# Attention slots with the two probability transposes half a slot apart, and the bias sums split

## The chip, the cores and the metric

One core of one Trainium2 chip. The metric is the device time of one launch in microseconds, the median of several runs.

## The reference

The input is x, 32 sequences of 256 rows of 128 numbers. The output is x plus two branches of its layernorm: attention and a mixture of experts. All is fp32.

```python
xn = layernorm(x)
out = x + attention(xn) + ffn(xn)

# attention, 16 heads of 64
Q = xn @ Wq + bq;  K = xn @ Wk;  V = xn @ Wv;  R = xn @ Wr + br      # R: 10 numbers per head and row
extra[b,h,t,p] = sum_n R[b,h,t,n] * b_nd[n, t-p]   where 0 <= t-p < 128, else the logit is -1e9
W = softmax(Q K^T / 8 + extra);   A = W V;   return A @ Wproj + bproj

# ffn: 8 experts of 512, the two best per row by router logits, gelu, softmax-weighted sum
```

The window makes each block of 128 query rows look at one or two blocks of 128 keys: per head 128 x 128 numbers for the first query block (t = 0) and 128 x 256 for the second (t = 1), 384 columns in all.

## The kernel before

After a preparation (weights turned and split, layernorm, routing) the kernel runs attention for sequences 0 to 15, then the expert blocks, then attention for sequences 16 to 31. Each pass of 16 sequences is written as a first sequence, a hardware loop of seven turns with two sequences each, a last sequence, and a tail of four slots.

**Slots.** A sequence has eight slots j, one per pair of heads. Each engine has a function `sequence` that writes out its own order of work; engines meet by semaphores alone. In slot j, TensorE (lines 1428 to 1444) does:

- `keys` (lines 1281 to 1283): queries and keys of pair j + 1, six matmuls, into the bank KEY_BANK. ScalarE copies them to `qk` (line 776).
- `units` at place 0: in slots 0, 2, 3 and 5 a quarter of the values ("v", copied by ScalarE to `val`, line 757), in slots 1 and 4 an "r" unit (copied to `r_raw` at line 763, rounded on POOL at line 641, remainder on VectorE at line 1064, called `weights` there).
- `logits` of pair j (line 1392) into one of two pairs of banks.
- in even slots `values` (line 1412), the product of turned probabilities and values for the quad of heads that ended with pair j - 3; in odd slots `outputs` (line 1422), its projection.
- `turn_probs` (line 1381), three transposes of one head's probabilities, for the first ("even") head of pair j - 2, into the one bank PT_BANK.
- `units` at place 1: a position unit "g" (line 1352), in every slot. VectorE copies it to `gst` (line 1057), SP writes that to memory and reads it back skewed as `extra` (lines 468 and 480), the bias for a later slot.
- `turn_probs` of the second ("odd") head of pair j - 2, into the same bank.

All v, r and g units share one bank, MISC_BANK, and wait for the copy of the unit before.

**VectorE** (lines 1077 to 1113) in slot j: reciprocal of the sums of pair j - 1 (line 1083); four reductions `tensor_tensor_reduce` (line 1093), which add `extra` to the logits and keep the minimum, two for t = 0, then two for t = 1; in odd slots `add_heads` (line 1122), the sum of an output quad; `copy_probs` (line 1073) of the even head of pair j - 2; the copy of the position unit; `copy_probs` of the odd head; in slots 1 and 4 `weights`. In the second pass `add_rows` (line 1136), four instructions, stands behind slots 1 and 2 and adds expert results.

`turn_probs` and `copy_probs` wait for each other, as there is one bank:

```python
pe.wait_ge(norm_made, 2 * (i * H + h + 1))     # turn_probs
wait_from(pe, pT_made, i * H + h)
...
dve.wait_ge(pT_psum, i * H + h + 1)            # copy_probs
wait_from(dve, head_psum, i * QUADS + h // 4)  # the values that read this buffer
```

**ScalarE** (lines 779 to 802) in slot j: copy of the keys; copy of the v or r unit; exponents of the pair (line 792), two for t = 0, two for t = 1, each with an accumulator read; in even slots the copy `headT` of the values' bank (line 801).

**POOL**: `split_q` for the next sequence in slot 0 (lines 630 to 635), the four scalings of pair j - 1 by its reciprocals (lines 666 and 668), and eight indirect DMAs per sequence (lines 651 and 653), which move rows to and from the experts. Its order and SP's are the same before and after.

## Time and profile before

| what | value |
|---|---|
| median of 3 runs | 1775.75 us (1775.34 to 1776.92) |
| profiled execution | 1773.52 us, of which the span is 1771.7 us |
| mean granted TensorE clock | 0.972 |
| busy over the span | TensorE 85%, VectorE 58%, ScalarE 54%, POOL 45% |
| two attention passes | about 137 to 810 us and 1087 to 1770 us |
| expert blocks | about 810 to 1087 us |

Times in the rows are microseconds from the start of the span unless marked ns. PE is TensorE's matmul side, PEld its weight loads, DVE is VectorE, ACT ScalarE, POOL GpSimd, SP SyncE. "Idle before" is time in which an engine did nothing ahead of an instruction, with the instruction that ended it behind the arrow; "issue" means that the profile shows no releaser. A wait on a register's value is often named so, whoever ended it.

### The profile page before, as it was taken

How to read it: one execution, taken by the hardware profiler on the slowest of the kernel's cores; microseconds unless marked ns; L12 is line 12 of the kernel's file. 1: busy time of each engine (PE TensorE's matmuls, PEld its weight loads, DVE VectorE, ACT ScalarE, POOL GpSimd, SP SyncE). 2: the span in 40 equal slices, each digit the busy share in tenths (PEclk: the TensorE clock that was granted, in tenths of full speed). 3: DMA queues.
4: the chain of work that ended last, by engine and by line, in shares of the span. 5: the costliest groups of instructions: out<-in, count | busy, mean ns of one | idle time of the engine just before them, and what ended most of it. 6: DMA issues, size and time to landing. Idle time of an engine off the chain costs nothing.

```text
span 1771.7 us, 43010 instructions
## 1 busy us (share of the span) xinstructions
PE 1497.9 (85%) x11335; PEld 1150.4 (65%) x11335; DVE 1026.8 (58%) x3715; ACT 956.8 (54%) x2864; POOL 804.7 (45%) x1515
## 2 busy tenths in 40 slices
PE   2556888888888888888999998888888888888886
PEld 1224666666666666667999996666666666666665
DVE  4675666666666666663212122676666766766675
ACT  1223566555666666664444453666665665655654
POOL 0323555655555555561000001555665565655554
PEclk8687999999999999999999998999999999999999
DMA  9765554545545554544666665555555555555541
GB/s 282 276 238 149 153 146 145 150 144 150 157 139 145 148 148 139 149 127 132 200 208 200 209 197 165 145 149 137 153 148 144 150 148 139 153 146 150 147 137 48
DMA packets 375831, 283.10 MB, mean 160 GB/s; under 512 B 16634, under 2 KB 349988, under 8 KB 375716
## 3 DMA queue, kind: packets, MB, share of 16 engines
q1 hardware_dynamic: 367524, 265.16, 50.7%
q0 software_dynamic: 8192, 16.79, 3.6%
q14 instruction: 90, 0.74, 0.1%
q8 instruction: 25, 0.41, 0.1%
HBM read 168.57 MB, written 113.26 MB: 159 GB/s over the span
## 4 chain that ended last, share of the span: by engine, by line
PE 61%; DVE 17%; issue 15%; SPq 4%; DMA 1%; DVEq 1%; POOL 0%; ACT 0%; POOLq 0%; ACTq 0%
PE ps L1381 11%; PE ps L1412 9%; PE ps L1317 8%; PE ps L1281 8%; PE ps L1392 7%; PE ps L1282 7%; PE ps L1283 7%; DVE probT L1073 7%; DVE logit L1093 5%; PE ps L1422 2%; DVE low L1093 1%; PE ps L1299 1%; SPq L435 1%; SPq L396 1%; PE ps L1352 1%
## 5 line engine op out<-in xcount | busy, mean ns | idle before, releaser
L792 ACT ACTIVATE prob<-logit,low 128x128 f32<-128x128 f32 (+1 forms) x1024 | 453.7, 444 | 264.0 <-DVE low L1093 260.1
L1093 DVE CUSTOM_DVE_ANT_0 logit<-ps,extra 128x128 f32<-128x128 f32 (+1 forms) x1024 | 306.3, 355 | 313.1 <-issue 237.9
L1381 PE MATMUL ps<-ident,prob 128*128 128x128 f32 x1536 | 265.7, 282 | 166.7 <-DVE probT L1073 145.1
L666 POOL TENSOR_SCALAR prob<-prob,inv 128x128 f32<-128x128 f32 x512 | 188.4, 368 | 437.9 <-DVE inv L1083 436.7
L1073 DVE COPY probT<-ps 128x384 f32<-128x384 f32 x512 | 284.3, 555 | 110.3 <-PE ps L1381 62.9
L1381 PEld LDWEIGHTS ps<-ident,prob 128*128 128x128 f32 x1536 | 165.1, 141 | 261.1 <-issue 200.1
L776 ACT COPY qk<-ps 128x512 f32<-128x512 f32 x256 | 150.0, 586 | 251.0 <-PE ps L1283 249.6
L668 POOL TENSOR_SCALAR prob<-prob,inv 128x256 f32<-128x256 f32 x512 | 241.2, 471 | 0.0
L1392 PE MATMUL ps<-qk 64*128 64x128 f32 (+1 forms) x2048 | 237.2, 350 | 0.0
L1412 PE MATMUL ps<-probT,val 128*64 128x256 f32 (+1 forms) x2048 | 194.7, 332 | 2.7 <-issue 1.4
L792 ACT ACTIVATION_READ_ACCUMULATOR prob<-logit,low 128x1 f32 x1024 | 191.5, 187 | 0.0
L1057 DVE COPY gst<-ps 128x512 f32<-128x512 f32 x256 | 174.4, 681 | 13.1 <-DMA skew<-gst 7.8
L1412 PEld LDWEIGHTS ps<-probT,val 128*64 128x64 f32 x2048 | 127.1, 136 | 81.5 <-issue 42.3
L1392 PEld LDWEIGHTS ps<-qk 64*128 64x128 f32 x2048 | 134.2, 186 | 65.1 <-ACT qk L776 36.0
L641 POOL CAST r_hi<-r_raw 120x512 fp32r<-120x512 f32 x64 | 39.0, 610 | 300.7 <-ACT r_raw L763 300.7
L1281 PE MATMUL ps<-xq_hi,wqk_hi 128*128 128x256 f32 x512 | 165.7, 324 | 1.4 <-ACT qk L776 1.4
L1422 PEld LDWEIGHTS ps<-wproj,headT 128*128 128x128 f32 x1024 | 123.9, 191 | 43.0 <-issue 41.2
L651 POOL DMA_INDIRECT x_place<-xrow,at_now x128 | 131.9, 1031 | 38.5 <-issue 25.3
L1422 PE MATMUL ps<-wproj,headT 128*128 128x128 f32 x1024 | 148.1, 288 | 1.4 <-ACT headT L801 1.4
L1317 PEld LDWEIGHTS ps<-w2b,hid 128*128 128x128 f32 x1248 | 145.2, 192 | 3.3
L653 POOL DMA_INDIRECT yget<-y_place,at_now x128 | 129.9, 1015 | 36.5 <-issue 24.9
L1317 PE MATMUL ps<-w2b,hid 128*128 128x128 f32 x1248 | 145.4, 275 | 0.0
(171 smaller groups left out, 2425.2 us busy)
## 6 DMA issues: line engine op xcount, KB each, us to landing
skew<-gst SPq DMA_DIRECT2D x256, 256.0 KB
extra<-skew SPq DMA_DIRECT2D x128, 512.0 KB, 3.8
extra<-skew SPq DMA_DIRECT2D x128, 256.0 KB, 2.9
w1b<-w_d SPq DMA_DIRECT2D x39, 514.0 KB, 3.5
w2b<-w_d SPq DMA_DIRECT2D x39, 320.0 KB, 3.3
x_place<-zero SPq DMA_DIRECT2D x39, 256.0 KB, 2.8
placed<-x_place SPq DMA_DIRECT2D x39, 256.0 KB, 3.7
y_place<-yrow SPq DMA_DIRECT2D x39, 256.0 KB, 2.2
```

What stands on the lines that cost most here:

```text
L666: nc.gpsimd.tensor_scalar(prob[:, h, 0:P], prob[:, h, 0:P], inv[:, h, 0:1], 1.0, ALU.mult, ALU.mult).then_inc(norm_made, 1)
L668: nc.gpsimd.tensor_scalar(prob[:, h, P:], prob[:, h, P:], inv[:, h, 1:2], 1.0, ALU.mult, ALU.mult).then_inc(norm_made, 1)
L792: ins = nc.scalar.activation(prob[:, h % PB, a:b], logit[:, h % LB, a:b], ACT.Exp, scale=-1.0, bias=low[:, h % LB, t:t + 1], accum_out=tot ...
L1057: nc.vector.tensor_copy(gst[:, t, :], ps[:, MISC_BANK, :]).then_inc(g_made, 1)
L1073: nc.vector.tensor_copy(probT[:, h % 4, :], ps[:, PT_BANK, 0:3 * P]).then_inc(pT_made, 1)
L1093: ins = nc.vector.tensor_tensor_reduce(out=logit[:, h % LB, a:b], in0=ps[:, S_BANK[j % 2][n], a:b], in1=extra[:, h, a:b], scale=1.0, scala ...
L1281: nc.tensor.matmul(dst, a_hi, b_hi, start=start, stop=False)
L1317: mm = nc.tensor.matmul(ps[:, Y_BANK[u], t * P:(t + 1) * P], hid[:, u, c, t * P:(t + 1) * P], w2b[:, u, c * P:(c + 1) * P], start=(c == 0) ...
L1381: mm = nc.tensor.transpose(ps[:, PT_BANK, n * P:(n + 1) * P], prob[:, h % PB, n * P:(n + 1) * P], ident[:, :])
L1392: mm = nc.tensor.matmul(ps[:, S_BANK[pair % 2][n], cols], qk[rows, pair % 2, 0, q], qk[rows, pair % 2, 1, k], start=True, stop=True)
L1412: mm = nc.tensor.matmul(ps[DQ * n:DQ * n + DQ, HEAD_BANK, q], val[:, s, v:v + DQ], probT[:, hh % 4, p], start=(s == 0), stop=(s == 1), ski ...
L1422: mm = nc.tensor.matmul(ps[:, HEAD_BANK, t * E:(t + 1) * E], headT[:, pair, t * P:(t + 1) * P], wproj[:, (2 * quad + pair) % PAIRS, :], st ...
```

## The change

Only the order of instructions on three engines changes; each instruction, bank and buffer stays.

- TensorE: logits of pair j; place-0 unit; transposes of the odd head of pair j - 3; keys of pair j + 1; position unit; transposes of the even head of pair j - 2; values or outputs.
- VectorE: `weights` of the slot before (so now in slots 2 and 5); copy of the odd head of pair j - 3; reductions for t = 0; reciprocal of pair j - 1; reductions for t = 1; copy of the position unit; copy of the even head of pair j - 2; `add_heads`; `add_rows`.
- ScalarE: place-0 unit; keys; exponents for t = 0; `headT`; exponents for t = 1.

```diff
@@ -776,23 +776,26 @@
                 nc.scalar.copy(qk[:, pair % 2, :, :].rearrange("p n k -> p (n k)"),
                                ps[:, KEY_BANK, :]).then_inc(key_made, 1)
 
+            def exponents(i, j, t):
+
+                a, b = ((0, P), (P, 3 * P))[t]
+                act.wait_ge(logit0_made if t == 0 else logit_made, i * PAIRS + (j + 1))
+                for h in (2 * j, 2 * j + 1):
+                    if t == 0:
+                        wait_from(act, pT_psum, i * H + (h + 1 - PB))
+                    ins = nc.scalar.activation(prob[:, h % PB, a:b], logit[:, h % LB, a:b], ACT.Exp,
+                                               scale=-1.0, bias=low[:, h % LB, t:t + 1],
+                                               accum_out=total[:, h % PB, t:t + 1])
+                return ins
+
             def sequence(i, start, heads=True, more=True):
                 for j in range(PAIRS if heads else LAG):
+                    for n, kind, k, t, ahead in units_at(j, 0, more) if heads else []:
+                        unit(len(START) + i * len(UNITS) + n, kind, k, t, i + ahead)
                     if heads and (j + 1 < PAIRS or more):
                         keys(i if j + 1 < PAIRS else i + 1, (j + 1) % PAIRS)
-                    for n, kind, k, t, ahead in units_at(j, 0, more) if heads else []:
-                        unit(len(START) + i * len(UNITS) + n, kind, k, t, i + ahead)
                     if heads:
-                        for t, (a, b) in enumerate(((0, P), (P, 3 * P))):
-                            act.wait_ge(logit0_made if t == 0 else logit_made, i * PAIRS + (j + 1))
-                            for h in (2 * j, 2 * j + 1):
-
-                                if t == 0:
-                                    wait_from(act, pT_psum, i * H + (h + 1 - PB))
-                                ins = nc.scalar.activation(prob[:, h % PB, a:b], logit[:, h % LB, a:b], ACT.Exp,
-                                                           scale=-1.0, bias=low[:, h % LB, t:t + 1],
-                                                           accum_out=total[:, h % PB, t:t + 1])
-                        ins.then_inc(prob_made, 1)
+                        exponents(i, j, 0)
                     if j % 2 == 0 and here(i, j - 4, heads, start):
 
                         quad = (j - 4) // 2
@@ -800,6 +803,8 @@
                         wait_from(act, out_psum, i * QUADS + quad)
                         nc.scalar.copy(headT[:, :, :].rearrange("p n t -> p (n t)"),
                                        ps[:, HEAD_BANK, :]).then_inc(head_made, 1)
+                    if heads:
+                        exponents(i, j, 1).then_inc(prob_made, 1)
 
             def experts(b, u, k):
                 if not isinstance(b, int) or b + 1 < PLACES:
@@ -1072,43 +1077,49 @@
                 wait_from(dve, head_psum, i * QUADS + h // 4)
                 nc.vector.tensor_copy(probT[:, h % 4, :], ps[:, PT_BANK, 0:3 * P]).then_inc(pT_made, 1)
 
+            def reduce(i, j, t):
+
+                a, b = ((0, P), (P, 3 * P))[t]
+                for n in range(2):
+                    h = 2 * j + n
+                    ins = nc.vector.tensor_tensor_reduce(
+                        out=logit[:, h % LB, a:b], in0=ps[:, S_BANK[j % 2][n], a:b], in1=extra[:, h, a:b],
+                        scale=1.0, scalar=BIG, op0=ALU.add, op1=ALU.min, accum_out=low[:, h % LB, t:t + 1])
+                ins.then_inc(logit0_made if t == 0 else logit_made, 1)
+
             def sequence(i, start, heads=True, more=True):
                 for j in range(PAIRS if heads else LAG):
-                    pair = j - 1
-                    if here(i, pair, heads, start):
-
-                        h = 2 * pair % PB
-                        dve.wait_ge(prob_made, i * PAIRS + pair + 1)
-                        wait_from(dve, norm_made, 2 * (i * H + 2 * pair + 2 - PB))
-                        nc.vector.reciprocal(inv[:, h:h + 2, :], total[:, h:h + 2, :]).then_inc(inv_made, 1)
+                    for n, kind, k, t, ahead in units_at(j - 1, 0, more) if heads else []:
+                        if kind == "r":
+                            weights(i + 1, k)
+                    if here(i, j - 3, heads, start):
+                        copy_probs(i, 2 * (j - 3) + 1)
                     if heads:
                         if j % 2 == 0:
                             wait_apart(dve, skew_in[j], (i + 1) * 16, const_made)
                             dve.wait_ge(skew_in[j + 1], (i + 1) * 16)
                         wait_apart(dve, s_psum, i * PAIRS + j + 1, const_made)
                         wait_apart(dve, prob_made, i * PAIRS + j + 1 - LB // 2, const_made)
-                        for t, (a, b) in enumerate(((0, P), (P, 3 * P))):
-                            for n in range(2):
-                                h = 2 * j + n
-                                ins = nc.vector.tensor_tensor_reduce(
-                                    out=logit[:, h % LB, a:b], in0=ps[:, S_BANK[j % 2][n], a:b], in1=extra[:, h, a:b],
-                                    scale=1.0, scalar=BIG, op0=ALU.add, op1=ALU.min, accum_out=low[:, h % LB, t:t + 1])
-                            ins.then_inc(logit0_made if t == 0 else logit_made, 1)
-                    if j % 2 == 1 and here(i, j - 5, heads, start):
-                        add_heads(i, (j - 5) // 2)
+                        reduce(i, j, 0)
+                    pair = j - 1
+                    if here(i, pair, heads, start):
+
+                        h = 2 * pair % PB
+                        dve.wait_ge(prob_made, i * PAIRS + pair + 1)
+                        wait_from(dve, norm_made, 2 * (i * H + 2 * pair + 2 - PB))
+                        nc.vector.reciprocal(inv[:, h:h + 2, :], total[:, h:h + 2, :]).then_inc(inv_made, 1)
+                    if heads:
+                        reduce(i, j, 1)
+                    for n, kind, k, t, ahead in units_at(j, 1, more) if heads else []:
+                        positions(len(START) + i * len(UNITS) + n, i + ahead, k, t)
                     if here(i, j - 2, heads, start):
                         if isinstance(i, int) and i == HALF and j == 2:
 
                             dve.wait_ge(y_out[0], (PLACES + 1) // 2 * 16)
                             dve.wait_ge(y_out[1], PLACES // 2 * 16)
                         copy_probs(i, 2 * (j - 2))
-                    for n, kind, k, t, ahead in units_at(j, 1, more) if heads else []:
-                        positions(len(START) + i * len(UNITS) + n, i + ahead, k, t)
-                    if here(i, j - 2, heads, start):
-                        copy_probs(i, 2 * (j - 2) + 1)
-                    for n, kind, k, t, ahead in units_at(j, 0, more) if heads else []:
-                        if kind == "r":
-                            weights(i + 1, k)
+                    if j % 2 == 1 and here(i, j - 5, heads, start):
+                        add_heads(i, (j - 5) // 2)
                     if j in ADDS and start == HALF and here(i, -1, heads, start) and heads:
                         add_rows(i - HALF - 1, ADDS.index(j), i - 1)
 
@@ -1427,21 +1438,21 @@
 
             def sequence(i, par, start, heads=True, more=True):
                 for j in range(PAIRS if heads else LAG):
+                    if heads:
+                        logits(i, j)
+                        units(i, par, j, 0, more)
+                    if here(i, j - 3, heads, start):
+                        turn_probs(i, 2 * (j - 3) + 1)
                     if heads and (j + 1 < PAIRS or more):
                         keys(i if j + 1 < PAIRS else i + 1, par if j + 1 < PAIRS else 1 - par, (j + 1) % PAIRS)
                     if heads:
-                        units(i, par, j, 0, more)
-                        logits(i, j)
+                        units(i, par, j, 1, more)
+                    if here(i, j - 2, heads, start):
+                        turn_probs(i, 2 * (j - 2))
                     if j % 2 == 0 and here(i, j - 4, heads, start):
                         values(i, (j - 4) // 2)
                     if j % 2 == 1 and here(i, j - 5, heads, start):
                         outputs(i, (j - 5) // 2)
-                    if here(i, j - 2, heads, start):
-                        turn_probs(i, 2 * (j - 2))
-                    if heads:
-                        units(i, par, j, 1, more)
-                    if here(i, j - 2, heads, start):
-                        turn_probs(i, 2 * (j - 2) + 1)
 
             for s0 in (0, HALF):
                 s1 = s0 + HALF
```

## Rows read from the trace of the kernel before

**Rows 1.** Timeline, POOL: start, us, engine, line, operation, of two loop turns' first instruction.
```profile
602.99 0.62 POOL L630 TENSOR_TENSOR xq<-xnT,one 128x256 f32<-128x256 f32 x1
...
685.69 0.62 POOL L630 TENSOR_TENSOR xq<-xnT,one 128x256 f32<-128x256 f32 x1
```

**Rows 2.** Busy by stage: stretch, length, busy of each engine, clock, DMA share, GB/s.
```profile
602.99:685.69 82.70, 72.51 (x576) 54.38 (x576) 52.64 (x205) 50.00 (x165) 48.46 (x92) 1.00 0.51 147
1218.39:1301.09 82.70, 72.50 (x576) 54.37 (x576) 57.16 (x222) 50.00 (x166) 48.35 (x92) 1.00 0.54 146
810.00:1087.00 277.00, 272.26 (x1926) 249.63 (x1926) 57.50 (x85) 131.96 (x199) 2.19 (x5) 1.00 0.61 192
```

**Rows 3.** Who waited for whom: us in total, times, longest us.
```profile
PE ps L1381 <- DVE probT L1073: 145.1, 224, 1.4
...
DVE inv L1083 <- issue: 32.7, 12, 3.0
...
PE ps L1381 <- issue: 19.0, 30, 0.7
```

**Rows 4.** Chain that ended last, in order of time: start, us, what.
```profile
590.15 0.23 PE ps L1281
...
590.85 0.86 PE ps L1392 x8
591.70 1.09 PE ps L1422 x8
592.79 0.33 PE ps L1381 x3
593.12 0.23 PE ps L1352
593.35 0.65 issue
...
594.51 0.12 PE ps L1281
...
596.08 1.48 PE ps L1412 x16
...
618.88 0.49 PE ps L1381 x3
```

**Rows 5.** Timeline of one slot, VectorE and TensorE; in brackets idle before, releaser.
```profile
623.03 0.29 DVE L1093 CUSTOM_DVE_ANT_0 logit<-ps,extra 128x128 f32<-128x128 f32 x1 [1.73 <-issue]
...
624.14 0.42 DVE L1122 TENSOR_TENSOR acc<-ps,acc 128x256 f32 x1
...
624.48 0.55 DVE L1073 COPY probT<-ps 128x384 f32<-128x384 f32 x1
...
624.94 0.68 DVE L1057 COPY gst<-ps 128x512 f32<-128x512 f32 x1
...
625.17 0.52 PE L1381 MATMUL ps<-ident,prob 128*128 128x128 f32 x3 [0.65 <-DVE probT L1073]
```

**Rows 6.** Timeline just behind VectorE's jump back at the loop's end.
```profile
607.09 0.18 DVE L1083 RECIPROCAL inv<-total 128x4 f32<-128x4 f32 x1 [2.85 <-issue]
...
607.65 0.29 DVE L1093 CUSTOM_DVE_ANT_0 logit<-ps,extra 128x128 f32<-128x128 f32 x1 [0.38 <-issue]
...
609.47 0.52 PE L1381 MATMUL ps<-ident,prob 128*128 128x128 f32 x3 [1.15 <-DVE probT L1073]
```

**Rows 7.** Lines 1064 and 1136: duration ns min/median/max, first and last start us.
```profile
L1064 DVE SCALAR_TENSOR_TENSOR rT<-r_hi,minus_low,r_raw x64: 741/744/1105, 140.8 to 1703.7; 120x512 fp32r<-120x512 f32 x64
...
L1136 DVE SCALAR_TENSOR_TENSOR acc<-yget,wtop,acc x128: 341/345/352, 1148.8 to 1768.6; 128x128 f32 x112, 128x128 f32<-128x128 f32 x16
```

**Rows 8.** Groups by shape, 400 to 800 us: busy, mean ns, idle before, releaser.
```profile
L792 ACT ACTIVATE prob<-logit,low 128x256 f32<-128x256 f32 x156 | 76.9, 494 | 0.0
L668 POOL TENSOR_SCALAR prob<-prob,inv 128x256 f32<-128x256 f32 x156 | 73.4, 470 | 0.0
...
L801 ACT COPY headT<-ps 128x512 f32<-128x512 f32 x39 | 21.9, 562 | 0.0
```

More of the change, by code:

```diff
@@ L1073, in copy_probs @@
                 nc.vector.tensor_copy(probT[:, h % 4, :], ps[:, PT_BANK, 0:3 * P]).then_inc(pT_made, 1)
+            def reduce(i, j, t):
[6 more added lines that the diff above has]
+                ins.then_inc(logit0_made if t == 0 else logit_made, 1)
             def sequence(i, start, heads=True, more=True):
                 for j in range(PAIRS if heads else LAG):
+                    for n, kind, k, t, ahead in units_at(j - 1, 0, more) if heads else []:
[4 more added lines that the diff above has]
+                    if heads:
+                        if j % 2 == 0:
+                            wait_apart(dve, skew_in[j], (i + 1) * 16, const_made)
+                            dve.wait_ge(skew_in[j + 1], (i + 1) * 16)
+                        wait_apart(dve, s_psum, i * PAIRS + j + 1, const_made)
+                        wait_apart(dve, prob_made, i * PAIRS + j + 1 - LB // 2, const_made)
+                        reduce(i, j, 0)
                     pair = j - 1
@@ L1084, in sequence @@
                     if heads:
-                        if j % 2 == 0:
-                            wait_apart(dve, skew_in[j], (i + 1) * 16, const_made)
-                            dve.wait_ge(skew_in[j + 1], (i + 1) * 16)
-                        wait_apart(dve, s_psum, i * PAIRS + j + 1, const_made)
-                        wait_apart(dve, prob_made, i * PAIRS + j + 1 - LB // 2, const_made)
-                        for t, (a, b) in enumerate(((0, P), (P, 3 * P))):
-                            for n in range(2):
-                                h = 2 * j + n
-                                ins = nc.vector.tensor_tensor_reduce(
-                                    out=logit[:, h % LB, a:b], in0=ps[:, S_BANK[j % 2][n], a:b], in1=extra[:, h, a:b],
-                                    scale=1.0, scalar=BIG, op0=ALU.add, op1=ALU.min, accum_out=low[:, h % LB, t:t + 1])
-                            ins.then_inc(logit0_made if t == 0 else logit_made, 1)
-                    if j % 2 == 1 and here(i, j - 5, heads, start):
-                        add_heads(i, (j - 5) // 2)
+                        reduce(i, j, 1)
+                    for n, kind, k, t, ahead in units_at(j, 1, more) if heads else []:
+                        positions(len(START) + i * len(UNITS) + n, i + ahead, k, t)
                     if here(i, j - 2, heads, start):
```

## Prediction

> **What bounds the kernel now.** I read the busy shares by stage first, then who waits for whom, then the chain of waits in order of time, then the timeline of single slots. POOL splits the next sequence's input once per sequence, so the same instruction recurs after two sequences, one turn of the loop: 82.70 us apart [rows 1], in the second pass as in the first [rows 2]. That is 5.17 us per slot of one head pair. In such a turn TensorE is busy for 72.5 of 82.70 us, VectorE for 53 or 57, ScalarE for 50, POOL for 48 [rows 2]: TensorE is nearest to its limit, and no other engine is near one. The granted clock is 1.00 there, the upper level of 2.4 GHz, and also 1.00 in the expert stage, where TensorE is busy for 272 of 277 us [rows 2]. So a denser TensorE has a precedent in this trace, and I charge nothing for the clock.
>
> What TensorE waits for is one thing. Its second transpose group of a slot (line 1381) waits for VectorE's copy of the first (line 1073), since both use one bank: 145.1 us in 224 waits, and 19.0 us in 30 more whose releaser the profile does not name [rows 3]. That is 254 waits for 256 head pairs, 0.65 us each. The chain shows one: outputs 1.09, first transposes 0.33, position unit 0.23, wait 0.65 [rows 4], second transposes 0.52 [rows 5]. A group that has waited takes 0.52, one that follows in the stream 0.33 [rows 4], so each wait also costs 0.19 of filling. In the timeline VectorE starts the copy at 624.48, after its four reductions and the sum, and TensorE starts 0.14 after the copy's end [rows 5]. Ahead of that VectorE itself sat idle for 1.73 us, waiting for the logits [rows 5].
>
> Check of this account, per sequence by the chain's durations [rows 4]: keys 8 x 6 x 0.12 = 5.76; value units 4 x 3 x 0.23 = 2.76; r units 2 x 6 x 0.12 = 1.44; position units 8 x 0.23 = 1.84; logits 8 x 0.86 = 6.88; values 4 x 1.48 = 5.92; outputs 4 x 1.09 = 4.36; first transposes four times 0.33 and, behind values, four times 0.49; second ones eight times 0.33: 5.92. Sum 34.9, two sequences 69.8. With 16 waits of 0.84 that is 83.2, against 82.70 seen. The account closes to 0.6%, so hardly anything else holds TensorE.
>
> **The change, part by part.** I count from the end of TensorE's slot, time 0.
> TensorE's new slot is logits 0.86, value or r unit 0.70, odd transposes 0.33, keys 0.72, position unit 0.23, even transposes 0.33, then values or outputs. Odd transposes end at 1.89. The copy starts 0.03 later, takes 0.56, and TensorE may go on 0.14 after it: 2.62. TensorE wants the bank at 1.89 + 0.72 + 0.23 = 2.84. Keys and position unit cover the copy by 0.2. The even transposes' copy has values or outputs, logits and mostly a unit (at least 1.95 us) as cover. In even slots that copy also waits for the values, because it overwrites their input: ready at 0.03 + 0.56 + 0.14 = 0.73, wanted at 0.86 even in the slots without a unit.
> **Gain:** 254 waits x 0.65 = 164 and 254 x 0.19 = 48, together 212. The six pairs in the two tails have no keys to cover them and keep theirs (6 x 0.84 = 5): 207.
>
> VectorE: weights and odd copy come first, then first reductions, reciprocal, second reductions, positions, even copy, sum. By starts and durations that is copy 0.46, all four reductions 1.11, positions 0.68, copy 0.46 [rows 5] and reciprocal 0.18 [rows 6]: 2.9, plus 0.34 for the sum in odd slots or 0.74 for weights [rows 7], in a TensorE slot of 69.8 / 16 = 4.36. It no longer waits for logits. The register waits before the first reductions cost 0.38 where only a 0.18 us reciprocal stands before them [rows 6]; behind the copy I take them as covered, as the position copy starts 0.46 after the probability copy although it too has waits [rows 5].
> **Loop ends:** VectorE's first instruction after a jump back starts 2.85 us after the last [rows 6]; 12 such gaps, six in each pass, make 32.7 us [rows 3], 2.7 each. Now that lands on the even transposes: sum 0.03 to 0.45 [rows 5], gap to 3.2, copy to 3.76, TensorE from 3.9 instead of 2.84, with filling 1.25; 12 x 1.25 = 15 back (0 if all is hidden, 12 x 3 = 36 if none). The present 1.15 wait there [rows 6] is within the 164. The Trainium skill (Advanced Engine Details and Errata, Control Flow Timing) puts a compare-and-branch at about 108 ns; the 2.85 us here disagree, and by the page's figure the 15 would be nothing.
> **Row sums of the second pass** (line 1136, four of 0.345 each [rows 7]) stand at the end of VectorE's slots 1 and 2. In slot 2: sum to 0.45, rows to 1.8, weights 0.74 [rows 7] to 2.5, odd copy to 3.1, TensorE from 3.2 instead of 2.84: 0.55 with filling, some 0.1 in slot 3; 15 x 0.65 = 10 back (0 to 20).
> Weights (line 1064) moves across a slot border, nearer to POOL's work. Its longest run is 1105 ns against a median of 744 [rows 7], so something can stretch it by 0.36; two per sequence have room for that except in the case above, 15 x 0.36 = 5, which I leave in the bound. The Trainium skill (Advanced Engine Details and Errata, GPSIMD Details) says that POOL shares a read and a write interface with VectorE and conflicts with instructions of two SBUF inputs, which line 1064 is. By that rule the sum would be 5 higher; by the median row it is not.
> ScalarE: unit copy first, key copy, first exponents, headT, second exponents. In even slots the second exponents now stand behind headT, which waits for values: 0.03 + 0.56, then 2 x 0.49 [rows 8] and what reads the accumulators, 0.2 as an estimate, done at 1.8. VectorE's reciprocal needs them only behind its first reductions, near 2.8. The next unit copy (0.6) ends at 2.4; TensorE's position unit wants it at 2.61. Cost nothing, with little slack: a lateness of 0.3 in the four even slots would be 32 x 4 x 0.3 = 38, the upper bound.
> POOL: reciprocal half a slot later, then two scalings of up to 0.47 per head [rows 8], well before the even transposes of the following slot; I charge nothing. Its moves, SP's writes and reads keep their order, and the skewed tiles are wanted two or more slots later: nothing.
> **New joints on TensorE** (values to logits, position unit to transposes, with two register waits behind 0.23 us of work): no row shows them. Nothing to 0.1 per slot; a gain is excluded since the durations above are already those without gaps. I take 0.05, 256 x 0.05 = 13.
> **Tails:** one more pair half lies behind the last logits: 2 x 1.5 = 3.
>
> Sum: -207 + 15 + 10 + 13 + 3 = -166. The profiled execution took 1773.5 (span 1771.7); minus 166 is 1607.5. The median of the runs is 2.2 higher, so 1610.
>
> **Rivals.**
> A, the forecast: the wait is gone and TensorE runs nearly without gaps. The closing account and idle VectorE speak for it. Own range 1588 (no joints, loop ends partly hidden) to 1648 (the bounds of ScalarE, joints and loop ends not all at once). Chance 0.73.
> B, the wait shrinks but stays. The cover is 0.2 only; if register waits keep VectorE's odd copy 0.5 late, TensorE waits 0.3 + 0.19. In half of the slots that gives back 128 x 0.49 = 63: 1673; in all of them 125: 1735. For it: 0.38 lost after the reciprocal [rows 6]. Against: 1.5 us of slack per slot. Chance 0.17.
> C, slower: VectorE becomes a ring. One slot's odd copy, reductions, reciprocal, positions and even copy in full durations, 0.56 + 1.4 + 0.18 + 0.68 + 0.56 = 3.4, with four uncovered register waits 4 x 0.38 = 1.5, then 0.14 + 0.52 + 0.03 through TensorE: 5.6 us against 5.17, +0.4 x 250 = 105, 1880. It decides from three uncovered waits up. Against it stands the position copy that starts before the copy ahead of it has ended [rows 5]. Chance 0.05.
> D, no change: the bank's wait only hid another of the same length, and the slot stays at 5.17: 1775. The closing account speaks against it. Chance 0.05: 0.03 within the bound below, 0.01 on either side of it.
>
> **Numbers.** 0.2% (3.5 us) is about what can be told from no change. Faster: A, B and 0.01 of D, 0.91; same: 0.03 of D; slower: C and 0.01 of D, 0.06. The range runs from A's low end to B's first value, 1588 to 1676; it leaves out B's upper half, C and D, and A's far low side.
>
> **What would show it.** Right: a loop turn of about 71 to 73 us instead of 82.70; line 1381's wait for line 1073 left at the loop ends, in slots 2 and 3 of the second pass and in the tails, below 40 us in all; TensorE busy for over 95% of a turn; the clock still 1.00; VectorE's wait for logits gone, and its new waits at line 1073 for transposes. Wrong: over 100 waits of line 1381 for line 1073 (B); VectorE without idle time (C); waits of position units for ScalarE's copies (its bound); a granted clock below 1.00 in the loops.

## The result, and the profile after

The new kernel takes 1595.92 us (median of 4 runs, 1594.13 to 1597.8) against 1775.78 us of the kernel before: a ratio of 0.8986, 95% interval 0.8971 to 0.9002. The profiled execution took 1594.13 us with a span of 1592.4. The forecast was 1610 us.

TensorE's share of the span is now 92%. The busy times by stage, with the same columns as [rows 2]; the first two stretches are again one loop turn each, from one POOL input split to the one after the next:

```profile
538.89:609.47 70.58, 69.80 (x578) 55.37 (x578) 51.26 (x204) 49.54 (x165) 48.69 (x93) 1.00 0.59 172
1182.18:1254.05 71.87, 70.66 (x578) 55.45 (x577) 55.37 (x220) 49.75 (x165) 48.56 (x92) 1.00 0.58 168
716.00:993.00 277.00, 272.31 (x1926) 249.67 (x1926) 57.41 (x85) 132.23 (x200) 1.86 (x4) 1.00 0.61 192
```

A turn takes 70.58 us in the first pass and 71.87 in the second instead of 82.70. TensorE is busy for 69.8 of the 70.58; the other engines do the same work in less time. The granted clock stays at 1.00 in all three stretches, its upper level, and the expert stage did not change. From the waits of the new kernel (us in total, times, longest):

```profile
DVE probT L1078 <- PE ps L1392: 155.8, 169, 1.5
...
DVE rT L1069 <- POOL r_hi L641: 20.0, 48, 1.3
PE ps L1392 <- DVE probT L1078: 18.0, 23, 1.1
...
PE ps L1363 <- DVE rT L1069: 10.5, 15, 7.2
```

Line 1392 is the old line 1381, line 1078 the old 1073. The 164 us of waiting of [rows 3] are now 18, and the wait has changed sides: VectorE, which has time, waits 156 us for TensorE's transposes. Of the 10.5 us of line 1363, the position unit, 7.2 are one wait at 140.7 us, ahead of the first pass's slots; the other 14 waits are of 0.24 each, all in the second pass. The chain of the new kernel in order of time, for one odd slot and the head of the next:

```profile
545.64 0.33 PE ps L1392 x3
545.97 0.89 PE ps L1433 x8
546.87 0.86 PE ps L1403 x8
547.72 0.43 PE ps L1292
548.15 0.23 PE ps L1293
...
548.62 0.33 PE ps L1392 x3
...
549.66 0.23 PE ps L1363
549.89 0.33 PE ps L1392 x3
550.22 1.45 PE ps L1423 x16
```

It is TensorE alone: even transposes 0.33, outputs 0.89, logits 0.86, a value unit 0.43 and twice 0.23, odd transposes 0.33, keys, position unit 0.23, even transposes 0.33, values 1.45. Against [rows 4] the extra time at the joints moved: outputs take 0.89 behind transposes and took 1.09 behind logits, and the even transposes take 0.33 behind the position unit where the first ones took 0.49 behind values; but the first product of a value unit takes 0.43 behind logits and took 0.23 behind keys, and in the two slots of a sequence that have no unit the odd transposes, now behind logits, take 0.48 (at 565.84 in the same chain). And how closely the copy is covered, in the timeline:

```profile
548.46 0.49 PE L1392 MATMUL ps<-ident,prob 128*128 128x128 f32 x3
...
548.98 0.56 DVE L1078 COPY probT<-ps 128x384 f32<-128x384 f32 x1
...
549.73 0.49 PE L1392 MATMUL ps<-ident,prob 128*128 128x128 f32 x3
```

Odd transposes end at 548.95, the copy runs from 548.98 to 549.54, and the even transposes begin at 549.73 with nothing marked as idle. That is 0.19 after the copy's end; a group that has waited begins 0.14 or 0.15 after it. Of the even groups of the whole trace 193 begin 0.18 or 0.19 after the end of their copy, 30 more 0.14 or 0.15 after it with an idle time too short to be marked: the cover is 0.05 longer than the copy needs, at most.

### The profile page after: what moved, and what is told of

Its sections match the earlier page's. It is cut to its first block, busy times and chain, and to the rows that moved or that the text cites. A ratio compares the mean times of both kernels' runs of the same rounds, so it can differ in the third digit from the quotient of the medians.

```text
span 1592.4 us, 42954 instructions
## 1 busy us (share of the span) xinstructions
PE 1466.6 (92%) x11335; PEld 1167.1 (73%) x11335; DVE 1002.3 (63%) x3715; ACT 950.5 (60%) x2864; POOL 809.0 (51%) x1515
## 4 chain that ended last, share of the span: by engine, by line
PE 78%; DVE 7%; issue 6%; SPq 5%; POOL 1%; DMA 1%; DVEq 1%; ACT 1%; POOLq 0%; ACTq 0%
PE ps L1403 12%; PE ps L1423 11%; PE ps L1392 11%; PE ps L1292 10%; PE ps L1328 9%; PE ps L1294 8%; PE ps L1293 8%; PE ps L1433 6%; PE ps L1363 3%; DVE logit L1085 1%; SPq L435 1%; DVE probT L1078 1%; PE ps L1310 1%; SPq L396 1%; DVE acc L1147 1%
## 5 line engine op out<-in xcount | busy, mean ns | idle before, releaser
L1085 DVE CUSTOM_DVE_ANT_0 logit<-ps,extra 128x128 f32<-128x128 f32 (+1 forms) x1024 | 315.1, 345 | 4.9 <-PE ps L1403 4.4
L1392 PE MATMUL ps<-ident,prob 128*128 128x128 f32 x1536 | 255.9, 275 | 19.1 <-DVE probT L1078 18.0
L1392 PEld LDWEIGHTS ps<-ident,prob 128*128 128x128 f32 x1536 | 174.3, 140 | 90.4 <-issue 40.3
L786 ACT ACTIVATION_READ_ACCUMULATOR prob<-logit,low 128x1 f32 x1024 | 194.7, 190 | 0.0
L1163 DVE TENSOR_TENSOR yrow<-ps,w2b 128x512 f32<-128x512 f32 x39 | 27.0, 692 | 190.0 <-PE ps L1328 190.0
L1293 PE MATMUL ps<-xq_lo,wqk_hi 128*128 128x256 f32 x512 | 144.9, 283 | 0.0
```

Source lines behind the costliest of these rows:

```text
L786: ins = nc.scalar.activation(prob[:, h % PB, a:b], logit[:, h % LB, a:b], ACT.Exp, scale=-1.0, bias=low[:, h % LB, t:t + 1], accum_out=tot ...
L1085: ins = nc.vector.tensor_tensor_reduce(out=logit[:, h % LB, a:b], in0=ps[:, S_BANK[j % 2][n], a:b], in1=extra[:, h, a:b], scale=1.0, scala ...
L1293: nc.tensor.matmul(dst, a_hi, b_lo, start=False, stop=False)
L1392: mm = nc.tensor.transpose(ps[:, PT_BANK, n * P:(n + 1) * P], prob[:, h % PB, n * P:(n + 1) * P], ident[:, :])
```

## The experiments

All ran in the same way beside the kernel before, and their ratios are to it; the differences in the text are to the new kernel's 1596.

**1. The two transpose groups side by side again**, TensorE alone.

```diff
                 for j in range(PAIRS if heads else LAG):
+                    if here(i, j - 3, heads, start):
+                        turn_probs(i, 2 * (j - 3) + 1)
                     if heads:
                         logits(i, j)
                         units(i, par, j, 0, more)
-                    if here(i, j - 3, heads, start):
-                        turn_probs(i, 2 * (j - 3) + 1)
...
-                    if here(i, j - 2, heads, start):
-                        turn_probs(i, 2 * (j - 2))
                     if j % 2 == 0 and here(i, j - 4, heads, start):
                         values(i, (j - 4) // 2)
                     if j % 2 == 1 and here(i, j - 5, heads, start):
                         outputs(i, (j - 5) // 2)
+                    if here(i, j - 2, heads, start):
+                        turn_probs(i, 2 * (j - 2))
```

> The new kernel with the two transpose groups side by side again: the even one behind values or outputs, the odd one at the head of the next slot, ahead of the logits. VectorE and ScalarE keep their new orders. Theory (the gain is the work that TensorE has between the two groups): each pair waits for the copy again, 0.03 + 0.56 + 0.14 = 0.73, and 0.19 of filling, about 250 x 0.9 = 225 us more than the new kernel's 1596, so about 1815, with over 200 waits of the transposes for the copy. Rival (the gain comes from VectorE's and ScalarE's new orders, TensorE's only had to follow): within 30 us of 1596.

Measured: 1878.37 us, ratio 1.0583 (1.0566 to 1.0601). Its waits:

```profile
PE ps L1392 <- DVE probT L1078: 192.5, 254, 1.4
```

254 waits of 0.76, with filling 241 us. The new kernel has 22 us of the same (23 waits), so 219 of the 282 us more are these. Another part shows in its chain: between the value or r unit and the position unit, which share a bank, there are now the keys alone to cover the unit's copy on ScalarE, and the position unit takes 0.46 to 0.56 instead of 0.23 (in the 12 slots of a turn that have a unit, 3 of the turn's 19 us):

```profile
516.08 0.59 ACT r_raw L763
...
516.72 0.50 PE ps L1363
```

So the transposes' second duty in the new order, standing between a unit and the next, counts too. VectorE's and ScalarE's new orders give nothing without it: with them and side-by-side transposes the kernel is 104 us slower than before. TensorE's order of before under the other two new ones was not run; this kernel keeps TensorE's new order in all but the transposes.

**2. VectorE's order of before** under TensorE's and ScalarE's new ones.

```diff
                 for j in range(PAIRS if heads else LAG):
-                    for n, kind, k, t, ahead in units_at(j - 1, 0, more) if heads else []:
-                        if kind == "r":
-                            weights(i + 1, k)
-                    if here(i, j - 3, heads, start):
-                        copy_probs(i, 2 * (j - 3) + 1)
...
                         copy_probs(i, 2 * (j - 2))
-                    if j % 2 == 1 and here(i, j - 5, heads, start):
-                        add_heads(i, (j - 5) // 2)
+                    for n, kind, k, t, ahead in units_at(j, 1, more) if heads else []:
+                        positions(len(START) + i * len(UNITS) + n, i + ahead, k, t)
+                    if here(i, j - 2, heads, start):
+                        copy_probs(i, 2 * (j - 2) + 1)
+                    for n, kind, k, t, ahead in units_at(j, 0, more) if heads else []:
+                        if kind == "r":
+                            weights(i + 1, k)
```

The reciprocal stands ahead of all four reductions and the sum behind them again, as in the kernel before.

> The new kernel with VectorE's order of before, TensorE's and ScalarE's new. Theory (half a slot apart is enough only if VectorE's copies are in TensorE's new order): the position copy now stands behind the even copy, which in even slots waits for the values at the end of TensorE's slot (time 0); even copy to 0.6, position copy to 1.3, and the value or r unit that wants its bank comes at 0.86: 0.5 of waiting and 0.25 of filling in slots 1, 3 and 5, 32 x 3 x 0.75 = 72 us more, about 1668 (1620 to 1720), with the idle time in front of the value and r units. Rival (TensorE's order alone gives the gain, VectorE follows by itself): 1596 to 1605.

Measured: 1810.4 us, ratio 1.0224 (1.0181 to 1.0267), 214 us more where 72 were expected. The place was right, the first product of the place-0 unit (line 1286), which waits for VectorE's position copy:

```profile
PE ps L1286 <- DVE gst L1062: 136.1, 150, 3.3
...
PE ps L1357 <- DVE rT L1069: 26.5, 29, 7.2
...
PE ps L1286 <- issue: 17.2, 28, 0.7
```

But it waits in all six slots with a unit, mostly 0.4 to 0.9 each, also behind odd slots, where I had seen no reason for it. The reason there is the output sum (line 1127), which stands ahead of the even copy in VectorE's old order and waits for the outputs, which TensorE's new order has at the end of its slot:

```profile
DVE acc L1127 <- PE ps L1427: 56.8, 83, 3.5
...
527.27 0.42 DVE L1127 TENSOR_TENSOR acc<-ps,acc 128x256 f32 x1 [0.43 <-PE ps L1427]
```

The even copy follows at 527.61, the position copy at 528.07, and the value unit waits 0.72 for it until 528.81. Further, a position unit waits 0.7 for the weights, and at the loop's end the jump stands between the odd copy and everything else:

```profile
533.95 0.18 DVE L1088 RECIPROCAL inv<-total 128x4 f32<-128x4 f32 x1 [3.25 <-issue]
...
536.10 0.68 DVE L1062 COPY gst<-ps 128x512 f32<-128x512 f32 x1
...
536.92 0.56 PE L1286 MATMUL ps<-xq_hi,wr_hi 128*120 128x256 f32 x1 [3.17 <-DVE gst L1062]
```

TensorE now waits 3.17 there, where the new order leaves 0.8, and behind it the granted clock falls. Busy by stage:

```profile
536.90:538.40 1.50, 1.48 (x7) 1.48 (x8) 0.00 (x0) 0.58 (x3) 0.00 (x0) 0.50 0.39 122
538.40:541.00 2.60, 2.60 (x16) 2.53 (x15) 1.73 (x10) 1.08 (x3) 0.96 (x3) 0.63 0.11 34
541.00:547.00 6.00, 4.36 (x33) 3.43 (x31) 3.42 (x11) 3.15 (x12) 1.69 (x5) 1.00 0.31 87
```

It stands at the lower level, 1.2 GHz, just after the gap and is back at the upper one 4 us later. In all, twelve stretches of 10 us lie below 1.00 in the slots of the two passes (none in the new kernel's loops), and they sum to 17 us of lost clock (10 us times what is missing to 1.00, over the twelve). Half a slot between the transposes is worth nothing without VectorE's order. Which part of that order carries how much was not taken apart; above all the split of the reductions, with the reciprocal between them, was never run by itself.

**3. ScalarE's order of before** under TensorE's and VectorE's new ones.

```diff
-                    for n, kind, k, t, ahead in units_at(j, 0, more) if heads else []:
-                        unit(len(START) + i * len(UNITS) + n, kind, k, t, i + ahead)
                     if heads and (j + 1 < PAIRS or more):
                         keys(i if j + 1 < PAIRS else i + 1, (j + 1) % PAIRS)
+                    for n, kind, k, t, ahead in units_at(j, 0, more) if heads else []:
+                        unit(len(START) + i * len(UNITS) + n, kind, k, t, i + ahead)
```

All four exponents of the pair stand ahead of headT again.

> The new kernel with ScalarE's order of before (keys ahead of the value or r unit, headT last). Theory: the copy of the unit now stands behind that of the keys, which end on TensorE 0.72 before the position unit's turn is due, so the position unit waits for keys end + 0.04 + 0.59 + 0.59 + 0.12 = 1.34 and 0.25 of filling in the six slots with a unit: 32 x 6 x 1.6 = 305 us more, about 1900. Rival (ScalarE is off the path, 60% busy, and its order is free): below 1610.

Measured: 1828.28 us, ratio 1.0304 (1.0287 to 1.0321), 232 more.

```profile
PE ps L1358 <- ACT val L757: 142.9, 122, 1.2
...
PE ps L1358 <- ACT r_raw L763: 70.9, 60, 1.3
```

182 waits of 1.17 at the position unit, 214 us: the mechanism as expected, the wait 0.17 shorter than the 1.34 foreseen. Most of that is in the two copies: I had added two full 0.59, but ScalarE starts the unit's copy 0.49 after the one of the keys (at 516.71 and 516.22, before a position unit at 517.35). An engine that is busy for 60% of the span still decides by its order.

**4. Exponents ahead of headT**, ScalarE otherwise as in the new kernel.

```diff
                     if heads:
                         exponents(i, j, 0)
+                        exponents(i, j, 1).then_inc(prob_made, 1)
                     if j % 2 == 0 and here(i, j - 4, heads, start):
...
-                    if heads:
-                        exponents(i, j, 1).then_inc(prob_made, 1)
```

> The new kernel with ScalarE's second exponents ahead of headT, as in the order before; keys and units stay in the new order. Theory: headT waits for the values at the slot's end anyway and the exponents are done by then, so nothing is lost: 1590 to 1600, the same within 0.3%. Rival (the change's place for headT between the exponents carries part of the gain, because outputs of the next slot wait for headT): 1605 or more, with waits of the outputs for headT.

Measured: 1597.62 us, ratio 0.8999 (0.8984 to 0.9014). No difference from the new kernel that can be told. This part of the change carries nothing.

**5. The odd head's copy twice**, the first time into a spare buffer.

```diff
+                if h % 2:
+                    nc.vector.tensor_copy(scrap[:, :], ps[:, PT_BANK, 0:3 * P])
                 nc.vector.tensor_copy(probT[:, h % 4, :], ps[:, PT_BANK, 0:3 * P]).then_inc(pT_made, 1)
```

> The new kernel with one more copy of the odd head's bank, into a buffer of its own, ahead of the real one: the copy that TensorE must cover takes 0.46 longer. Theory (cover of keys and position unit 0.2, which is just the filling that a wait costs, so no slack): about 0.43 lost for each of some 250 pairs, 108 us more than 1596, about 1704, with a wait of 0.2 to 0.3 in front of the even transposes in nearly every slot. Rival (VectorE and TensorE have room for another half microsecond): below 1620.

Measured: 1713.02 us, ratio 0.9651 (0.9636 to 0.9665), 117 us more where 108 were expected.

```profile
PE ps L1395 <- DVE probT L1081: 93.8, 251, 1.6
```

One of them in the timeline:

```profile
547.18 0.52 PE L1395 MATMUL ps<-ident,prob 128*128 128x128 f32 x3 [0.26 <-DVE probT L1081]
```

In 193 of the 251 it is 0.26 (the median 0.27) of waiting and 0.19 of filling: 0.45 for a copy that is 0.46 longer. The others are longer, up to 1.6; among them are those at the loop ends and in the tails, which the new kernel has too, shorter. In all the loss is 117 us over 251 waits, 0.47 each, so the new kernel's cover has no reserve that this run can find.

**6. Four sequences in a loop turn**, two ahead of the loop.

```diff
-                with pe.Fori(0, HALF // 2 - 1) as m:
-                    sequence(2 * m + (s0 + 1), 1, s0)
-                    sequence(2 * m + (s0 + 2), 0, s0)
+                sequence(s0 + 1, 1, s0)
+                sequence(s0 + 2, 0, s0)
+                with pe.Fori(0, HALF // 4 - 1) as m:
+                    sequence(4 * m + (s0 + 3), 1, s0)
...
+                    sequence(4 * m + (s0 + 6), 0, s0)
```

> The new kernel with four sequences in a loop turn instead of two, and two sequences ahead of the loop: 4 jumps back instead of 12 on TensorE, VectorE, ScalarE and POOL. Theory (a jump costs VectorE 2.7 and TensorE 0.84 of waiting and 0.19 of filling): 8 x 1.03 = 8 us less, 1588 (1584 to 1591). Rival (the longer body costs as much in fetching code in the middle of a turn, or the wait is not the jump's): 1594 or more.

Measured: 1606.89 us, ratio 0.9042 (0.9028 to 0.9055), 11 more instead of 8 less.

```profile
PE ps L1415 <- issue: 12.1, 4, 3.4
...
PE ps L1404 <- DVE probT L1086: 6.5, 10, 0.8
```

One of the four of line 1415, in the timeline:

```profile
541.13 1.65 PE L1415 MATMUL ps<-qk 64*128 64x128 f32 x8 [3.41 <-issue]
```

The busy times by stage behind it, with the granted clock at its lower level:

```profile
542.00:544.00 2.00, 2.00 (x7) 1.10 (x6) 0.00 (x0) 0.00 (x0) 0.72 (x2) 0.50 0.32 51
```

At the four jumps that are left TensorE itself stops for about 3 us, ahead of the logits (line 1415), which it never did with two sequences in the loop: 12 us in all. Behind three of the four the granted clock falls to 0.50 for some time, 1.2 GHz, 8 us lost by the same reckoning as in run 2. Against these 20 stand the waits for the odd copy, 6.5 us in 10 where the new kernel has 18.0 in 23, with filling 14 saved. That leaves 6 of the measured 11. Its trace has 5 us in further waits of TensorE that the new kernel's has not, of 1.5 us at most (1.0 to 1.4 ahead of value units at 1209.8, 1358.3 and 1507.6); what causes them stays open.

**7. The second pass's row sums behind the odd copy.**

```diff
+                    if j - 1 in ADDS and start == HALF and here(i, -1, heads, start) and heads:
+                        add_rows(i - HALF - 1, ADDS.index(j - 1), i - 1)
                     if heads:
                         if j % 2 == 0:
...
-                    if j in ADDS and start == HALF and here(i, -1, heads, start) and heads:
-                        add_rows(i - HALF - 1, ADDS.index(j), i - 1)
```

> The new kernel with the row sums of the second pass (line 1147) behind the odd copy of the slot after, instead of ahead of weights and odd copy. Theory (in slot 2 they make the weights late, and the position unit waits 0.24 for them, with filling 0.5): 15 x 0.5 = 7 us less, 1589 (1586 to 1593), no waits of 0.24 at line 1363, and the loop turn of the second pass 70.7 like that of the first. Rival (the sums only push the reductions back by 1.1, so exponents, position copy and the next unit come late, or POOL's wait for the sums grows until its scalings are late): 1598 or more.

Measured: 1617.44 us, ratio 0.9108 (0.9096 to 0.9121), 21 more. The rival is right:

```profile
1059.60 0.38 PE L1292 MATMUL ps<-xq_hi,wr_hi 128*120 128x256 f32 x1 [0.45 <-DVE gst L1062]
...
1064.04 0.69 DVE L1062 COPY gst<-ps 128x512 f32<-128x512 f32 x1 [1.37 <-DMA skew<-gst]
...
1064.78 0.51 PE L1292 MATMUL ps<-wv_hi,xq_hi 128*128 128x512 f32 x1 [0.30 <-DVE gst L1062]
```

The row sums take 1.13 and the position copy comes that much later; the next unit waits 0.45, so there had been some 0.65 of room. In the next slot the position copy waits 1.37 for the DMA that empties its buffer, and further on in that slot of TensorE the even transposes wait 0.5 (14 waits of line 1392, 13 of them in the second pass, whose releaser isn't named). So each sequence of the second pass has three new waits, 1.2 us together before filling, in place of the one of 0.24.

**8. Edits 6 and 7 together**, with both diffs.

> Both of the last two edits together. Theory: the two losses are in different slots and add: 15 us less than the new kernel, 1581 (1577 to 1585). Rival (they hide each other): 1586 or more.

Measured: 1626.9 us, ratio 0.9158 (0.9145 to 0.9172), 31 more: the times of the two losses add (11 + 21), so their independence held as foreseen, but both are losses and not gains.

**9. Half of the first row sums behind the odd copy.** From the room of 0.65 in run 7.

```diff
+                    if j - 1 == ADDS[0] and start == HALF and here(i, -1, heads, start) and heads:
+                        add_rows(i - HALF - 1, 0, i - 1, 1)
...
-                        add_rows(i - HALF - 1, ADDS.index(j), i - 1)
+                        add_rows(i - HALF - 1, ADDS.index(j), i - 1, 0 if j == ADDS[0] else None)
...
-                for t in range(PER):
+                for t in {None: range(PER), 0: range(2), 1: range(2, PER)}[part]:
```

> The new kernel with the first row sums of the second pass split: two of the four stay at the end of slot 1, two go behind slot 2's odd copy. Theory (whole row sums behind the odd copy cost because the position copy came 1.1 late and the next unit waited 0.45, so 0.65 of room is there; two take 0.56): weights come 0.56 earlier, the 0.24 waits at line 1363 are gone, nothing else is late, 15 x 0.5 = 7 us less, 1589 (1586 to 1592). Rival (room is less in a slot in which position copies wait for the DMA of the gst buffer): 1596 or more, with waits of value and r units for the position copy.

Measured: 1588.78 us, ratio 0.8962 (0.895 to 0.8973). The kernel before ran at 1772.65 beside it, so the ratio is what compares: 0.0024 below the new kernel's, 4 us, with intervals that just touch. One turn of its second pass:

```profile
1183.23:1254.22 70.99, 70.11 (x578) 55.37 (x577) 55.26 (x220) 49.73 (x165) 48.52 (x92) 1.00 0.60 171
```

70.99 us instead of 71.87, 0.44 per sequence or some 6 us over the pass (an estimate from this turn), near the 7 expected, and no wait at the position unit for weights is left in the loops. This is the lowest ratio of all runs.

**10. The output sums behind the odd copy of the next slot.**

```diff
                         copy_probs(i, 2 * (j - 3) + 1)
+                    if j % 2 == 0 and here(i, j - 6, heads, start):
+                        add_heads(i, (j - 6) // 2)
...
-                    if j % 2 == 1 and here(i, j - 5, heads, start):
-                        add_heads(i, (j - 5) // 2)
```

> The new kernel with the sum of an output quad (line 1133) not at the end of the odd slot but behind the odd copy of the slot after. Theory (VectorE's jump begins when its last instruction ends: now that is the even copy, 0.7 earlier; and in slot 2 the weights come 0.34 earlier): 12 x 0.7 = 8 us less at the loop ends, waits there of 0.1 to 0.3 instead of 0.8, and 15 x 0.5 = 7 us less at line 1363, together 1581 (1577 to 1585). Rival (VectorE's gap is tied to TensorE's slot, or the sum pushes the reductions so far that the next value or r unit waits): 1594 or more.

Measured: 1618.3 us, ratio 0.9132 (0.911 to 0.9155), 22 more by the times and 26 by the ratios. In the first pass the waits at the loop's end did fall, to between 0.36 and 0.73. In the second this comes once per sequence:

```profile
1059.40 0.40 SPq L575 DMA_DIRECT2D out_dram<-acc  x1
...
1062.88 0.69 DVE L1062 COPY gst<-ps 128x512 f32<-128x512 f32 x1 [2.69 <-DMA skew<-gst]
...
1063.63 0.50 PE L1295 MATMUL ps<-wv_hi,xq_hi 128*128 128x512 f32 x1 [1.95 <-DVE gst L1062]
```

SP's queue holds the store of a finished group (line 575) until a certain output sum is made; behind it stands the write of the gst buffer. With the sum later, the position copy waits 2.69 for the buffer and TensorE 1.95. Part of the loss is clock: the five times lie between 1613.5 and 1631.84, and the profiled execution is the longest of them. TensorE waits about 1.9 in 14 sequences of its second pass; behind ten of the waits the granted clock falls to 0.50 for some 3 us, behind the other four it doesn't. Behind a wait that ends at 1260 and one that ends at 1299:

```profile
1260.00:1263.00 3.00, 3.00 (x13) 2.67 (x12) 1.82 (x8) 0.59 (x1) 0.01 (x1) 0.50 0.96 259
1299.00:1302.00 3.00, 3.00 (x23) 2.72 (x24) 2.73 (x13) 1.66 (x5) 0.55 (x2) 1.00 0.85 230
```

By the reckoning of run 2 that is about 17 us in this execution. What decides whether the clock falls, this trace doesn't show.

**11. Edits 9 and 10 together**, with both diffs.

> Both of the last two edits. Theory: they take away the same wait at line 1363, so the second adds nothing to add_late: 1581, the same as add_late within 3 us. Rival: slot 2 of the second pass now holds sum and half of the row sums behind the odd copy, 0.9, more than its room of 0.65, and the next unit waits 0.25 in 15 sequences: 4 to 7 us above add_late.

Measured: 1616.54 us, ratio 0.9138 (0.9115 to 0.9162): the same as run 10, and like it some 35 us above the 1581 foreseen. The loss at the buffer, which is in both, hides what either theory says of slot 2. Its profiled execution (1615.96) has the same 14 waits of 1.9, with the clock at its lower level behind only one of them.

**12. Run 9, and the output sums late except that of slot 1.** Against run 11:

```diff
-                    if j % 2 == 0 and here(i, j - 6, heads, start):
+                    if j in (0, 4, 6) and here(i, j - 6, heads, start):
                         add_heads(i, (j - 6) // 2)
...
                         copy_probs(i, 2 * (j - 2))
+                    if j == 1 and here(i, j - 5, heads, start):
+                        add_heads(i, (j - 5) // 2)
```

> rows_split, and the sums of the output quads behind the odd copy of the next slot as in add_late, but not that of slot 1, which stays at that slot's end. Theory (add_late lost its gain because SP's queue stands at the store of a finished group until the sum of slot 1 is made, and behind it stands the write of the gst buffer): the 2.7 us waits of the position copy for the DMA and the 1.9 us waits of the value units in the second pass are gone, the loop ends keep their 0.4 instead of 0.8, 12 x 0.4 = 5 us less than rows_split, a ratio to the kernel before of 0.893 (0.890 to 0.895). Rival (sums behind the odd copy hurt the second pass by themselves, wherever they are): 0.905 or more, with waits of value or r units for the position copy.

Measured: 1614.55 us, ratio 0.9109 (0.9097 to 0.9122). The gain at the loop ends of the first pass is there (waits of 0.6 at most), but the loss of run 10 too:

```profile
1056.98 0.40 SPq L575 DMA_DIRECT2D out_dram<-acc  x1
...
1060.48 0.69 DVE L1062 COPY gst<-ps 128x512 f32<-128x512 f32 x1 [2.70 <-DMA skew<-gst]
...
1061.23 0.51 PE L1302 MATMUL ps<-wv_hi,xq_hi 128*128 128x512 f32 x1 [1.97 <-DVE gst L1062]
```

The same place in run 9:

```profile
1060.07 0.40 SPq L575 DMA_DIRECT2D out_dram<-acc  x1
...
1063.42 0.69 DVE L1062 COPY gst<-ps 128x512 f32<-128x512 f32 x1 [0.88 <-DMA skew<-gst]
```

From POOL's input split (at 1037.55 and 1042.28 in these two) to the store it is 19.4 us here and 17.8 in run 9, and the position copy waits 2.70 against 0.88. I had kept the wrong sum: the store's count, `QUADS * (n + HALF + 1)`, is reached with the sum of slot 3, which this kernel still moves. That a kernel that keeps the sum of slot 3 in place gains 5 us was not tried.

## Why the prediction was right

- **The bound, and the gain.** Right. With the wait of each pair under cover, a loop turn fell by 12.1 us in the first pass; by the terms it was to be 16 x 0.84 less a loop end of 1.25, 12.2. The signs that were named are there too: turns of 70.58 and 71.87 us, TensorE busy for 98 to 99% of them, 18 us left of the wait, the clock at 1.00. Runs 1 and 5 show the cause from both sides: put the groups together and 254 waits of 0.76 are there, lengthen the copy by 0.46 and 0.45 comes back per pair.
- **The margin.** The step said that keys and position unit cover the copy by 0.2. The margin is 0.05 at most in the new trace, and run 5 finds none. The sum compared 2.62, where a waiting group may start, with 2.84, where the position unit ends; but a group that follows in the stream starts 0.16 before that end (549.73 against 549.66 + 0.23). That the copy just fitted is luck as far as this sum goes, and rival B was nearer than its chance said: by run 5's figures, an estimate, a copy or a semaphore 0.1 slower would have cost some 25 us.
- **VectorE and ScalarE.** Costed at nothing in their new orders, rightly (run 4 for headT). But the prediction has no term and no rival for what their orders are worth. Runs 2 and 3 show each to be worth over 200 us under TensorE's new order.
- **New joints.** Taken at 0.05 each, 13 us. In the sum there are none: TensorE is busy for 69.80 us in a turn of the first pass, and the account with the old durations gave 69.8. The joints did cost, but no more than the old ones. Per sequence six units and two groups of transposes now lose 0.2 and 0.15 behind logits, 1.5 us; before, four outputs lost 0.2 behind logits and four groups of transposes 0.16 behind values, 1.4. That the two balance was not foreseen. This is the largest part of the difference between 1610 and 1596.
- **Loop ends.** Forecast 12 x 1.25 = 15. In the new kernel TensorE waits there 0.75 to 1.07 in the twelve cases, 10.5 us in all, with filling 12.7:

```profile
607.95 0.41 DVE L1133 TENSOR_TENSOR acc<-ps,acc 128x256 f32 x1
...
610.50 0.56 DVE L1078 COPY probT<-ps 128x384 f32<-128x384 f32 x1 [2.13 <-issue]
...
611.21 0.52 PE L1392 MATMUL ps<-ident,prob 128*128 128x128 f32 x3 [0.78 <-DVE probT L1078]
```

  VectorE's gap from its sum's end (608.36) to the odd copy is 2.13, less than the 2.7 taken.
- **Row sums.** Forecast 0.65 per sequence of the second pass; the two turns differ by 1.29, 0.65 per sequence. The place was in part another: the weights come late, and the position unit waits 0.24 for them and pays as much for filling. The even transposes behind it lose only 0.19: in slot 2 they start at 1193.72, 0.14 after the late copy ends, with an idle time too short to be marked. Together that is the 0.65. The size was right, its make-up was not.
- **Weights beside POOL's work.** Left in the bound, and it didn't come. Line 1064 is now line 1069:

```profile
L1069 DVE SCALAR_TENSOR_TENSOR rT<-r_hi,minus_low,r_raw x64: 735/753/1105, 139.8 to 1531.9; 120x512 fp32r<-120x512 f32 x64
```

  The two long ones, 1105 and 1086 ns, run at 140.4 and 993.4 us, ahead of each pass's slots, as in the kernel before; all others take 774 ns or less.
- **Tails.** Forecast 3 us more, not seen: from the last input split to the end less two turns' sequences it is 97.3 - 82.7 = 14.6 us before and 85.5 - 71.9 = 13.6 after.
- **What is left.** Joints, loop ends and tails together come out 19 us better than their terms, the time only 14 better than the forecast. Where the other 5 went was not traced.

## What to carry to other kernels

When an engine waits for the emptying of a bank that it has just filled, put independent work between the two fills, and count the cover against the copy, the semaphores' time and the pipeline's filling, here 0.56 + 0.17 + 0.19 = 0.92 against keys and position unit of 0.95. A new order on the busiest engine is worth only what the other engines' orders let through: move the copies into the order in which that engine will ask for the banks, also on engines that are busy for only 60%. Before moving a sum or a store by a slot, look up which count of it a DMA queue waits for and what stands behind that wait in the queue.

## What the runs showed of the hardware

- A group of full-array products takes 0.15 to 0.2 us longer behind the 64-row products of the logits, whether it is outputs (1.09 against 0.89), a unit (0.43 against 0.23 for its first product) or transposes (0.48 against 0.33). Transposes behind the values, whose products write 64 columns, take 0.16 longer (0.49).
- TensorE's jump back shows no gap of its own with two sequences in the loop's body and one of 2.8 to 3.4 us with four (run 6), VectorE's 2.1 to 3.4 with two (before and after the change, and in runs 1 to 5, 7 and 9).
- The granted clock fell to its lower level, 1.2 GHz, behind eight of TensorE's twelve waits of 3.0 to 3.3 us in run 2, behind three of the four of 2.8 to 3.4 in run 6, and behind ten of fourteen of about 1.9 in one execution of run 10, but one of fourteen in run 11; it stayed at the upper level behind the waits of about 1 us at the new kernel's loop ends.
- On the jumps, the Trainium skill (Advanced Engine Details and Errata, ISA Cache) gives TensorE a larger instruction cache than the other engines, 128 KB against 32; the runs agree in that TensorE was the one without a gap until its body doubled, but no run here measures the size of a body against a cache.
